# Counting a graph's edges by spans of five destinations, fetched from DRAM into two slots each, in a two-layer GNN kernel

## What is computed

```python
h = maximum(layernorm(x), 0)                      # then the T5 norm inside the first layer
out = h @ W_root + bias
for r in range(2):                                # type of edge
    w = (edge_type == r)
    sums = segment_sum((h[src] @ W_rel[r]) * w[:, None], dst, N)
    cnt = segment_sum(w, dst, N)
    out = out + sums / maximum(cnt, 1)[:, None]
x = x + (h + elu(out) @ wo)                       # first layer
g = maximum(layernorm(x), 0) @ W                  # second layer
e = exp(-leaky_relu((g @ a_l)[src] + (g @ a_r)[dst]))
h2 = segment_sum(e[:, None] * g[dst], src, N) / (segment_sum(e, src, N)[:, None] + eps)
x = x + elu(h2)
```

## Time and profile before

| | us |
|---|---|
| median of 3 runs | 555.28 |
| lowest and highest run | 555.07, 557.53 |
| profiled execution | 556.9 |
| its span | 555.1 |
| granted PE clock, mean | 0.996 of full |
| PE, DVE, ACT, POOL busy | 527.4, 396.7, 225.3, 75.1 |

### The profile page before, as it was taken

The page is one execution under the profiler, slowest core; times in us unless marked ns, Lnnn a source line. Parts: engine busy times, 40 slices in busy tenths (PEclk is TensorE's granted clock), DMA queues, the critical chain, the costliest instruction groups (busy, mean ns, idle before and its releaser), DMA issues.

```text
span 555.1 us, 8077 instructions
## 1 busy us (share of the span) xinstructions
PE 527.4 (95%) x3093; PEld 454.1 (82%) x3094; DVE 396.7 (71%) x662; ACT 225.3 (41%) x418; POOL 75.1 (14%) x69
## 2 busy tenths in 40 slices
PE   3989999999799999999999999999999999999996
PEld 3889898988788888989877888888778888888885
DVE  4837858559999898997586555655489887777633
ACT  5764335125754544444863332223132332222302
POOL 2372113000000000000000000000016232222410
PEclk9999999999899999999999999999999999999999
DMA  9862331313021123222395111110003232222221
GB/s 262 216 194 83 109 105 38 111 27 79 1 75 57 57 62 125 75 76 75 109 343 185 37 38 37 39 37 2 0 1 105 81 99 69 68 67 74 72 74 40
DMA packets 19805, 47.25 MB, mean 85 GB/s; under 512 B 3908, under 2 KB 8387, under 8 KB 19636
## 3 DMA queue, kind: packets, MB, share of 16 engines
q1 hardware_dynamic: 19761, 46.67, 27.7%
HBM read 31.30 MB, written 15.36 MB: 84 GB/s over the span
## 4 chain that ended last, share of the span: by engine, by line
PE 79%; DVE 9%; ACT 6%; DMA 3%; issue 2%; SPq 0%; DVEq 0%; ACTq 0%
PE ps L1186 10%; PE ps L1438 9%; PE ps L1440 8%; PE ps L1439 8%; PE ps L1347 8%; PE ps L1419 5%; PE ps L1421 5%; PE ps L1420 5%; PE ps L1304 5%; DMA wg_raw<-in_L_gnn_W 2%; PE ps L1390 2%; PE ps L1392 2%; PE ps L1391 2%; ACT counts L569 1%; PE ps L1402 1%
## 5 line engine op out<-in xcount | busy, mean ns | idle before, releaser
L1438 PE MATMUL ps<-h_hi,att_hi 125*125 125x512 f32 (+1 forms) x190 | 73.5, 387 | 0.0
L1439 PE MATMUL ps<-h_lo,att_hi 125*125 125x512 f32 (+1 forms) x190 | 72.6, 382 | 0.0
L1440 PE MATMUL ps<-h_hi,att_lo 125*125 125x512 f32 (+1 forms) x190 | 72.5, 382 | 0.0
L1419 PE MATMUL ps<-wg,gT_hi 128*125 128x512 f32 x160 | 64.0, 400 | 1.2 <-DVE wg L993 1.1
L1421 PE MATMUL ps<-wg,gT_lo 128*125 128x512 f32 x160 | 63.0, 394 | 0.0
L1420 PE MATMUL ps<-wg,gT_hi 128*125 128x512 f32 x160 | 63.0, 394 | 0.0
L1347 PE MATMUL ps<-msg_hi,adj_hi 125*125 125x288 f32 x200 | 56.7, 307 | 0.0
L547 ACT CAST adj_hi<-ps 125x400 fp32r<-125x400 f32 (+1 forms) x65 | 32.0, 492 | 59.0 <-PE ps L1304 59.0
L1347 PE MATMUL ps<-msg_lo,adj_hi 125*125 125x286 f32 x200 | 51.6, 297 | 0.0
L1186 PE MATMUL ps<-w_hi,hT_hi 128*125 128x430 f32 x128 | 46.4, 362 | 0.1
L1186 PE MATMUL ps<-w_hi,hT_lo 128*125 128x430 f32 x128 | 45.9, 358 | 0.0
(11 more groups left out here) (216 smaller groups left out, 1139.0 us busy)
## 6 DMA issues: line engine op xcount, KB each, us to landing
xt<-in_x SPq DMA_DIRECT2D x10, 448.0 KB
xh_scratch<-xt SPq DMA_DIRECT2D x10, 448.0 KB
xt<-xh_scratch SPq DMA_DIRECT2D x10, 448.0 KB
x_scratch<-xt SPq DMA_DIRECT2D x10, 448.0 KB
x1t<-x_scratch SPq DMA_DIRECT2D x10, 448.0 KB
xr<-x_scratch SPq DMA_DIRECT2D x10, 448.0 KB
out_x<-xr SPq DMA_DIRECT2D x19, 224.0 KB
wg_raw<-in_L_gnn_W SPq DMA_DIRECT2D x8, 512.0 KB, 9.4
```

The lines of the kernel that those rows point to most:

```text
L1419: M.matmul(to, hi, wg[k][:, 0, cut], start=n == 0, stop=False)
L1438: M.matmul(to, hi[:, s, :], h_hi[:, s, cut], start=s == 0, stop=False)
L1439: M.matmul(to, hi[:, s, :], h_lo[:, s, cut], start=False, stop=False)
L1440: return M.matmul(to, lo[:, s, :], h_hi[:, s, cut], start=False, stop=s == TILES - 1)
```

## The change

The windows are halved to 5 destinations, 250 of them, and a matmul has 100 columns. A window's edges are no longer taken chunk by chunk: DVE packs each edge's key and source into one number (`listed`), SP writes them as one list to DRAM, and copies from it 1296 overlapping rows of 256 edges, one beginning at every 32nd edge (`spread_list`). PE and DVE work out where each window's edges begin (`picks`, `picked`, `spans_of_windows`), POOL fetches for each window the row that begins at most 31 edges ahead of it (`gather_windows`, two indirect DMAs of 125 rows), PE transposes the rows into 2 slots of 128 edges a window (`windows_transposed`), and DVE unpacks them (`window_keys`). Edges in the slots that are another window's get a key outside 0 to 99 and so an empty one-hot row. A window's edges that are found are counted; if any of all E is missing (`missing`), a slow path counts everything over all 330 chunks. On the fast path a group is five windows (25 destinations, one PSUM bank of 500 columns): 10 matmuls of 100 columns, five groups a tile. The three lists of the fast path are reordered, and one-hot rows use all 128 partitions.

```diff
-    WD = 10
+    WD = 5
...
-    FIXED = 4
+    SLOTS = 2
...
-    RING, MORE = 3, 2
+    RING, MORE, FIRST = 4, 2, 2
...
+    GW = 5
+    NG = T // (GW * WD)
+    GC = GW * WC
...
+    STEP, SPAN, SPANS = 32, SLOTS * P, 1296
...
             for k, ap in enumerate((src, dst, edge_type)):
                 sp.dma_start(edges_i[:, k], ap.rearrange("(g p e) -> p g e", g=CG, p=CP)).then_inc(S["edges_in"], 16)
+            last_of = lambda first, n: bass.AP(dst.tensor, dst.offset + first * CP * T - 2, [[T, CP], [CP * T, n], [1, 2]])
+            sp.dma_start(last_i[1:CP, 0:1, :], last_of(0, 1)[1:CP]).then_inc(S["last_in"], 16)
+            sp.dma_start(last_i[:, 1:CG, :], last_of(1, CG - 1)).then_inc(S["last_in"], 16)
...
+            def store_list():
+                sp.wait_ge(S["list_rdy"], 1)
+                sp.dma_start(list_dram[0:E].rearrange("(g p e) -> p g e", g=CG, p=CP), comb[:]).then_inc(S["list_out"], 16)
+                sp.wait_ge(S["more_consts"], 1)
+                sp.dma_start(list_dram[E:LISTED].rearrange("(o e) -> o e", o=1), nothing[:]).then_inc(S["list_out"], 16)
+
+            def spread_list():
+                sp.wait_ge(S["list_out"], 32)
+                sp.dma_start(spans_dram[:], bass.AP(list_dram.tensor, list_dram.offset, [[STEP, SPANS], [1, SPAN]])).then_inc(S["spans_out"], 16)
+                sp.dma_start(xlist[:], list_dram[0:E].rearrange("(p c) -> p c", c=CHUNKS)).then_inc(S["xlist_in"], 16)
             for t in range(AHEAD, TILES):
                 store_xh(t, t % 2)
                 if t + 2 < TILES:
                     load_x(t + 2, t % 2)
+                if t == 5:
+                    store_list()
+                if t == 6:
+                    spread_list()
...
+            def gather_windows():
+                pool.wait_ge(S["span_rdy"], 1)
+                pool.wait_ge(S["spans_out"], 16)
+                for h in range(2):
+                    G.indirect_dma_start(win[:, h, :], None, spans_dram[:], bass.IndirectOffsetOnAxis(span_of[:, h:h + 1], 0)).then_inc(S["win_in"], 16)
...
-            pipeline((residual, 0), steps=(AHEAD, TILES))
+            pipeline((residual, 0), steps=(AHEAD, TILES - 2))
+            gather_windows()
+            pipeline((residual, 0), steps=(TILES - 2, TILES))
...
-                pipeline((counted(0), 0), (y_split, 2), (counted(1), 0), (counted(2), 0), (counted(3), 0),
-                         (counted(4), 0), (counts_part(0), 1), (elu, 1), (counted(5), 0), (counts_part(1), 1), (counted(6), 0), (counts_part(2), 1), opening=split_wo, before=2, steps=(0, TILES))
+                pipeline((counted(0), 0), (y_split, 2), (counted(1), 0), (counts_part(0), 1), (counted(2), 0), (elu, 1), (counts_part(1), 1),
+                         (counted(3), 0), (counts_part(2), 1), (counted(4), 0), opening=split_wo, before=2, steps=(0, TILES))
...
+            def window_keys():
+                dve.wait_ge(S["wkeyp_rdy"], 1)
+                by_slot = lambda ap: ap.rearrange("p (w j) -> p j w", j=SLOTS)
+                two = lambda ap: ap.rearrange("p (j w) -> p j w", j=SLOTS)
+                link(unpacked(lambda k: link(V.tensor_tensor(by_slot(wkey[:, 0]), k, two(woff[:]), ALU.add)),
+                         by_slot(wkey[:, 1]), two(bank(7, P, SLOTS * WINDOWS)), two(kk[:, 0])))
+                link(V.tensor_scalar(kk[:, 1], wkey[:, 0], 0.0, None, ALU.is_ge))
+                link(V.scalar_tensor_tensor(kk[:, 2], wkey[:, 0], float(WC), kk[:, 1], ALU.is_lt, ALU.mult))
+                V.tensor_reduce(found[:], kk[:, 2], AX, ALU.add).then_inc(S["found_rdy"], 1)
+                dve.wait_ge(S["found_rdy"], 1)
...
-                pipeline((one_hots(0), 0), (one_hots(1), 0), (z_of, 2), (one_hots(2), 0), (y_of, 2), (output1, 3), (one_hots(3), 0),
-                         (lambda t, b, d: split_wo() if t == 0 else None, 2), (one_hots(4), 0), (y_split, 2), (one_hots(5), 0), (one_hots(6), 0),
-                         steps=(0, TILES))
+                pipeline((one_hots(0), 0), (one_hots(1), 0), (y_split, 3), (one_hots(2), 0), (z_of, 2), (one_hots(3), 0), (y_of, 2),
+                         (one_hots(4), 0), (lambda t, b, d: split_wo() if t == 0 else None, 2), (output1, 3), steps=(0, TILES))
...
-            stage1(AHEAD, 7)
-            whole_keys()
-            stage1(7, 8)
-            spans()
-            stage1(8, 9)
-            tables()
-            stage1(9, 10)
-            window_keys()
+            stage1(AHEAD, 8)
+            picked()
+            stage1(8, 10)
+            windows_transposed()
             stage1(10, 11)
...
+            def windows_transposed():
+                pe.wait_ge(S["win_in"], 32)
+                for j in range(SLOTS):
+                    for h in range(2):
+                        at = j * WINDOWS + h * T
+                        last = M.transpose(ps[:, 7, at:at + T], win[:, h, j * P:(j + 1) * P], ident[0:T, 0:T])
                 last.then_inc(S["wkeyp_rdy"], 1)
...
+            def count_group(t, b, g):
+                n = nth(t, g)
+                pe.wait_ge(S["win_out"], bank_free(n))
+                pe.wait_ge(S["hot_ready"], n + 1)
+                for x in range(GW):
+                    for c in range(SLOTS):
+                        wide, srcs = (hots(n)[:, x, cut].rearrange("p (j k) -> p j k", k=SLOTS)[:, :, c] for cut in (slice(0, WIDE), slice(WIDE, HOT)))
+                        last = M.matmul(win_bank(n, x), srcs, wide, start=c == 0, stop=c == SLOTS - 1)
+                last.then_inc(S["hot_used"], 1)
...
-                pipeline((counted(0), 0), (y_transposed, 2), (counted(1), 0), (summed(0), 1), (counted(2), 0), (summed(1), 1),
-                         (counted(3), 0), (output1(0), 2), (counted(4), 0), (output1(1), 2), (counts_part(0), 1), (counted(5), 0),
-                         (counts_part(1), 1), (counted(6), 0), (counts_part(2), 1), steps=(0, TILES))
+                pipeline((counted(0), 0), (y_transposed, 2), (summed(0), 1), (counted(1), 0), (summed(1), 1), (counts_part(0), 1), (counted(2), 0),
+                         (output1(0), 2), (counts_part(1), 1), (counted(3), 0), (output1(1), 2), (counts_part(2), 1), (counted(4), 0), steps=(0, TILES))
```

More of the change, by code:

```diff
@@ L260, in pipeline @@
                         stage(s - lag, (s - lag) % 2, (s - lag) // 2)
-        def entry(eng, which, w, top):
-            return nc.s_assert_within(
-                eng.value_load(table[0:1, bass.ds(w + which * WINDOWS, 1)]), 0, top,
-                skip_runtime_bounds_check_because="the table is worked out on the chip within these bounds")
         def beyond_flag(eng):
-            return eng.to_reg(entry(eng, 3, 0, WINDOWS * CHUNKS))
+            return eng.to_reg(nc.s_assert_within(
+                eng.value_load(table[0:1, 0:1]), 0, E, skip_runtime_bounds_check_because="edges that are not found, of E"))
         @block.sync
@@ L688, in _ @@
                 with act.Fori(0, TILES // 2) as d:
[L689 to L693 removed]
+                    for b in range(2):
+                        for g in range(NG):
+                            counts_evicted(d * 2 + b, b, g)
                     for b in range(2):
@@ new lines, in picks @@
+            def picks():
+                dve.wait_ge(S["more_consts"], 1)
+                dve.wait_ge(S["last_in"], 32)
+                V.tensor_copy(qb[:, :, 0:T], quot[:, 0])
+                V.tensor_reduce(most[:], quot[:, 0], AX, ALU.max)
+                link(V.tensor_copy(last_q[:, 0], last_i[:, :, 1]))
+                floors(last_q[:, 1], last_q[:, 0], WD)
+                for g in range(CG):
+                    last = V.tensor_scalar(below[:, g], iw[:], last_q[:, 1, g:g + 1], None, ALU.is_gt)
+                link(last)
+                for g in range(CG):
+                    last = V.scalar_tensor_tensor(pick[:, g], iw[:], most[:, g:g + 1], below[:, g], ALU.is_le, ALU.mult)
+                last.then_inc(S["picks_rdy"], 1)
@@ L870, in first_rows @@
             def first_rows(groups):
-                with dve.If_eq(flags["dve"], 0):
-                    for p in groups:
-                        rows_of(0, p, RING + MORE)
+                for n in groups:
+                    rows_of(n)
             def stage1(first, end):
@@ L1216, in window_keys @@
-            def window_keys():
-                pe.wait_ge(S["picks_rdy"], 1)
-                for n, parts in enumerate(((0, 1), (2,))):
-                    for g in range(CG):
-                        for k in parts:
-                            last = M.matmul(bank(6 + n, T, NS), keyb[:, k, g], pick[:, g], start=(g == 0 and k == parts[0]),
-                                            stop=(g == CG - 1 and k == parts[-1]))
+                        last = M.matmul(ps[0:T, 6, P * h:P * h + T + 2], pick[:, g, T * h:T * (h + 1)], qb[:, g, 0:T + 2], start=g == 0, stop=g == CG - 1)
```

403 lines of the change are left out of this document (169 added, 234 removed).

## The result

| | before | changed |
|---|---|---|
| median | 555.80 us (4 runs, 555.07 to 557.53) | 533.51 us (4 runs, 532.65 to 534.85) |
| profiled execution, its span | 556.9 us, 555.1 us | 534.85 us, 533.0 us |
| ratio | 1 | 0.9597, 95% interval 0.9565 to 0.9629 |

Measured once more beside the last experiments, the changed kernel took 534.86 us (5 runs, 534.78 to 537.18), ratio 0.9628, interval 0.9608 to 0.9648. So two medians of the same kernel lie 1.35 us apart, and a gain of about a microsecond is not settled by one pair of medians. The forecast was 533.6 us, and 535.2 for the profiled execution. The total is right to 0.4 us; the parts are less so, as the rest shows.

A forecast was written before the change was run, and what follows sets the result against it. PE was taken to bound the kernel, with DVE close behind in the steps. Gains of 3.0, 3.4, 15.3 and 0 sum to 21.7 us: 556.9 to 535.2 profiled, median 533.6 us, range 527 to 543.

The forecast's parts named there:

- Price of a matmul: Count matmuls on PE: 100 columns take 50 ns each (45 to 57), so a group of ten 0.50 us.
- rival A: Count matmuls: price doesn't fall with columns and stays 90 ns; steps 2 to 9 cost 16 us more, 549.6; chance 0.08.
- Stage 1: Edge preparation on PE, 36.6 to 122.6 us: 4.2 us removed, 0.9 added, 0.3 taken off; gain 3.0 us.
- The thinnest cover: DVE's window keys in stage 1: next low parts end at about 109.2, PE wants them at 109.9.
- Steps 0 and 1: First two counting steps, first count to step 2's first count: 17.1 us where 20.5 stood, gain 3.4.
- I leave the low clock in on both sides: After the idle time at step 2's start the clock falls as before, costing 1.5 us before and after.
- Steps 2 to 9: Later counting steps: 13.3 us each, 108.9 in all with low clock and wo's split, from 124.2; gain 15.3 us.
- The 1.0 us for wo's split in step 2: Step 2: wo's split keeps DVE from y's low part, 1.0 us added on top of 1.5 of low clock.
- The end of layer 1: x1, wg loads and transposes hang on the last sums and move with them: gain 0.
- B: Waits on two banks, evictions of 500 columns and busy DVE replace the work: 1 us more a step, 541.6; chance 0.14.
- C: Stage 1: spread copy on one of 16 DMA engines takes 62 us, PE idles 38 us: 571; chance 0.04.
- D: An edge is not found, so all 50 groups go over all 330 chunks: over 5 ms; chance 0.01.

The follow-up runs named there:

- the longer chain: Changed kernel with four more passes of 500 elements in DVE's chain of window keys in stage 1: 539.35 us.
- the filler: Changed kernel with the first step's count matmuls issued twice per group, the tenth group's five times, to fill PE's waits: 534.19 us.
- early table: Changed kernel with ACT loading the exponent's table in step 1, ahead of its second group: 532.44 us.
- late fp16 copy: Changed kernel with the first tile's fp16 copy made once in step 1 from SBUF, not at each eviction: 530.68 us.
- DVE's added work: Changed kernel with one more unused DVE pass of 500 elements ahead of each one-hot group from the ninth on: 533.84 us.

## Why the prediction was right, step by step

- **Price of a matmul: right.** Forecast 50 ns (45 to 57), measured 45 to 47 at 100 columns and 27 at 50. I had left a margin for a floor from the weight load; none binds at 100 columns. The figure of the Trainium skill ("TensorE: Matmul & The Clock Gate", section "Back-to-back issue gap"), about 81 ns at 128 columns, doesn't hold for this stream; measurement decides, and rival A with it is out.
- **Stage 1: right, 3.6 us for 3.0.** 0.3 of the difference lies ahead of the stage and is scatter (it begins at 36.30 in this profile, 36.65 in the second one, 36.63 before). All covers held: the list was sent at 65.4, the spread copy at 70.9, landing 7.6 us later at 78.5 (my bounds 75 and 99, taken 85), the gather at 89.7 (I had 90). The thinnest cover was rightly named, and tighter than I had it: low parts done at about 109.1, PE ready at 109.3 (I had 109.2 and 109.9). A delay there costs more than itself, as the longer chain showed.
- **Steps 0 and 1: the step that failed, 0.8 us for 3.4.** The order of events was as forecast: evictions of 0.48 us, the sums from 6.3 us behind the first count on (I had 6.0), the wait ahead of step 2's first count (2.57 us). What failed is "I leave the low clock in on both sides", 1.5 us. It fell twice, also among the first counts, where PE, now faster, idles between ACT's evictions. The first sums took 4.90 us for 2.7, so 2.2 us here, which with the 0.3 of the later sums is the whole miss; those of step 2, 4.44, cost 1.7, nearly the forecast 1.5. A group now costs PE 0.47 us and ACT's two evictions 0.95, where it was 0.72 and 0.78: this made the idle time behind which the clock falls, and with that time filled, by counts issued twice or by the filler, it did not fall there.
- **Steps 2 to 9: right in kind, 17.1 us for 15.3.** A step is 13.2 for 13.3. The wait is the one forecast, at its place and from its releaser, 0.33 us for 0.4. The 1.0 us for wo's split in step 2 did not come on top of the low clock: no wait for DVE shows there in the changed kernel's first profile, and the product starts 0.15 us late in its second. Where the clock stayed up (early table, late fp16 copy, filler), PE waited 1.00 to 1.05 us for it. The two terms overlap, and I had added them; that is 1.0 of the 1.8, and steps of 13.2 for 13.3 nearly all the rest.
- **The end of layer 1: 0.6 us for 0.** It does not hang on the last sums alone: the load of the second layer's weights stands in the chain before (12.2 us), in that of the changed kernel's second profile and of seven experiments (12.3 to 14.2), and not in the changed kernel's first one. Where it does, the next transposes come a microsecond or two later behind the last sums. So the 0.6 is in part the luck of this profile, and a part of every gain ahead of it can be lost to it.
- So the wrong sizes, -2.6 and +1.8, and the two small ones, +0.6 each, left 0.4 of 22.1. That they cancelled is luck: the total was better than its parts.
- **Rivals.** A is refuted by the group's 0.47 us, B by DVE's added work and by the steps' length (its one true part is ACT's eviction, priced at 0.33). C was far off: the copy landed 7.6 us after its issue, where C had 62, and had about 13 us to spare. D didn't come: the flag led into the short way.

## What to carry to other kernels

When a matmul gets cheaper, look at the engine that empties its result bank: the bound stays PE only where PE isn't made to wait for the last eviction, and a semaphore on exactly what the next matmul reads can save a wait in every step (0.45 us here). A wait of two microseconds on PE is to be priced with the clock that may fall behind it, and costs that cover one another are not to be added: with the clock up, the next wait shows. Follow a gain through to the next transfer that is issued late: here a part of every gain in layer 1 went into the load of layer 2's weights.

## What the runs showed of the hardware

- bf16 matmuls with 128 columns of weights each run at 27 ns for 50 columns, 45 to 47 for 100 and 90 for 200: nearly by the columns, with no floor above 27 ns.
- A wait of 2.5 us of PE amid work at full clock was followed by a granted clock of 0.79 from 111 to 119 us, 1.5 us more of cost; behind waits of 1.1 to 1.5 and up to four of 0.2 to 0.6 us among the first counts the clock fell in five of eight profiles.
- A DRAM to DRAM copy of 1296 rows of 1 KB, overlapping by design, landed 7.6 to 7.9 us after its issue. Two gathers of 125 such rows held POOL for 1.39 and 1.21 us, and landed 3.9 to 4.2 us after the start of their issue.
